# Graph attention on one core: 32x32 block transposes on VectorE, and P times V in sixteen parts of the array

## Chip, cores, metric

One core of one Trainium2 chip. The metric is device time in microseconds (us) of the whole kernel, one launch. All tensors are in float32.

## What is computed

Two layers on x (16 batches, 512 nodes, 128 features), each followed by a residual and a layer norm.

```
h = x @ fc_in_w.T + fc_in_b                      # layer 0: 8 Euler steps on the graph
8 times: h = h + dt * (sigmoid(alpha)*0.5*(adj @ h - h) + h @ w_eff - h + x)
x1 = layernorm(x + h)
q, k, v = split_heads(x1 @ W)                    # layer 1: 4 heads of 32
P = softmax(q @ k.T / sqrt(32) + mask)           # mask: adj == 0 -> -inf; 512 x 512 per head
out = layernorm(x1 + P @ v)
```

## The kernel before

The eight Euler steps are folded into powers of one 512x512 matrix that is built once, in the first 60 us. After that the kernel works on one batch per iteration, 16 iterations, two of them (j = 0 and 1, one group of two batches) in one pass of the loop over g. Four jobs are software-pipelined: an iteration runs a share of layer 0 ("HORNER" pieces XT, Z, C, BC, BM), prepares the batch of two iterations ago (LN1A, LN1B, X1T, Q, K, V and the scores S0 of head 0), does the scores and transposes (S, TR) of the batch of three iterations ago, and ends the batch of four iterations ago (PV, OT, CB, LN2A, LN2B, and the store). The order in which every engine takes these is one hand-written list, EVENTS (L66), and LATE_EVENTS (L87) once layer 0 is through. All engines walk the same list in order, and each has only its own part of each event.

Attention, for one head (32 columns) and one of four tiles i of 128 queries:

- `S` (scores, L648): TensorE writes 128 queries by 512 keys to psS[i % 2]. VectorE (maximum, L847) adds the mask, takes the row maximum and writes the result to Sm; ScalarE (exponential, L461) writes exp to E[:, h % 2, i], queries on the partitions.
- `TR` (L702): P times V needs keys on the partitions, so TensorE transposes four 128x128 squares of E into a bank psE; ScalarE (L514, even i) or VectorE (L886, odd i) copies the bank to ET. An iteration has 16 TR, 64 transposes in all.
- `PV` (L717): for each of four key tiles n and each head, one matmul of 128 keys by 32 columns of V against 512 queries of ET. The four heads lie in four column groups of the array (psO[rows]). A float32 matmul is two loads and two matmuls for the engine, a transpose one of each; so an iteration has 32 PV pairs of load and matmul, and 64 transpose pairs.
- `OT` and `CB` bring psO back to queries on the partitions, and scale it by the reciprocal sums.

VectorE also makes the low parts of split float32r operands (L824) and the layer norms (L826 to L843), GpSimd the inverse roots (L400). SyncE's queue loads x, stores y, and stacks Q and K parts by 24 DMAs per iteration (L345), each 64 KB. V is kept by ScalarE (L506) in two buffers V[:, j]. The loop over g from 2 to 6 is one body that is run five times; the rest is unrolled.

Of the kernel before, what the change touches and what calls it, by code (L numbers as in the profile page):

```python
# [31 lines left out]
KS = 3 * HD  # L32

# [37 lines left out]
    ("HORNER", 2, 0),  # L71
# [7 lines left out]
    ("HORNER", 6, 0),  # L79
    ("TR", 3, 0), ("TR", 3, 1), ("S0", 0, 0), ("S0", 0, 1),  # L80
    ("HORNER", 7, 0), ("V", 3, 0),
    ("TR", 3, 2), ("TR", 3, 3), ("S0", 0, 2), ("S0", 0, 3),
# [67 lines left out]
def gnn_kernel(nc, x, adj, alpha, w, d, fc_w, fc_b, w_qkv, out):  # L150
    with ExitStack() as ctx:
# [42 lines left out]
        V = sb("V", [P, 2, NT, D])  # L194
# [735 lines left out]
```

## Time and profile before

| | us |
|---|---|
| three runs | 734.71, 736.24, 736.66 (median 736.24) |
| the profiled execution, its own time | 734.45 |
| its span | 732.4 |
| TensorE matmul busy | 687.3 (94%) |
| TensorE weight load busy | 558.1 (76%) |
| VectorE busy | 417.4 (57%) |
| ScalarE busy | 380.7 (52%) |

The span is the part between the first and the last recorded instruction; some 2 us lie around it. Busy times of different engines overlap, and weight loads lie beside matmuls. What sets the time is the engine that never waits in a stretch, so stretches of one iteration are read by themselves.

### The profile page before, as it was taken

To read this page: it belongs to the slowest core of one execution; us is meant where nothing else is said; L and a number is where in the kernel's file an instruction comes from. 1 tells how busy PE (TensorE), PEld (TensorE's weight loads), DVE (VectorE), ACT (ScalarE), POOL (GpSimd) and SP (SyncE) were. 2 spreads that over 40 slices of the span, in tenths; PEclk is the share of its full clock that TensorE was granted. 3 is DMA by queue.
4 is the path that set the end of the run, shared out by engine and by line. 5 is a ranking of instruction groups with operands and counts; after the bars stand their busy time and mean duration, and the time that the engine had idled before them with its cause. 6 is when DMAs were issued, how large, how long until landed. Compare 5 with 4: busy or idle time off the path is not lost.

```text
span 732.4 us, 14091 instructions
## 1 busy us (share of the span) xinstructions
PE 687.3 (94%) x4753; PEld 558.1 (76%) x4753; DVE 417.4 (57%) x1229; ACT 380.7 (52%) x855; POOL 71.1 (10%) x85
## 2 busy tenths in 40 slices
PE   5999999999999999999999999999999999978674
PEld 3778988987888788878797788878887889654441
DVE  5440114555576475657575667557564757686863
ACT  3131124665556565556565555656456655665660
POOL 5010100201002000200020100200020000000000
PEclk9999999999999999999999999999999999997997
DMA  3000003030302221130304030312112120312210
GB/s 104 1 1 29 1 30 84 15 98 9 92 12 71 59 58 42 43 86 25 75 0 124 5 96 4 80 49 63 37 47 55 34 69 23 80 40 62 76 27 29
DMA packets 37058, 35.39 MB, mean 48 GB/s; under 512 B 7456, under 2 KB 24224, under 8 KB 37024
## 3 DMA queue, kind: packets, MB, share of 16 engines
q1 hardware_dynamic: 37024, 34.96, 18.4%
q8 instruction: 19, 0.31, 0.2%
q14 instruction: 15, 0.12, 0.1%
HBM read 5.57 MB, written 4.19 MB: 13 GB/s over the span
## 4 chain that ended last, share of the span: by engine, by line
PE 75%; DVE 7%; issue 6%; SPq 5%; DMA 4%; ACT 2%; DVEq 0%; POOLq 0%; POOL 0%; ACTq 0%
PE psL L614 12%; PE psE L714 12%; PE psO L725 8%; PE psS L654 7%; SPq L345 5%; PE psL L625 4%; PE psL L627 4%; PE psL L626 4%; PE psL L642 3%; PE psL L644 3%; PE psL L643 3%; DMA Ks<-kl 3%; PE psM L691 3%; DVE Sm L855 2%; DVE y L843 2%
## 5 line engine op out<-in xcount | busy, mean ns | idle before, releaser
L466 ACT ACTIVATE E<-Sm,negmax 128x512 f32<-128x512 f32 x256 | 182.8, 716 | 137.3 <-DVE negmax L855 137.3
L855 DVE CUSTOM_DVE_ANT_0 Sm<-psS,mask 128x512 f32<-128x512 f32 x256 | 166.3, 684 | 14.9 <-PE psS L654 9.9
L886 DVE COPY ET<-psE 128x512 f32<-128x512 f32 x116 | 79.8, 688 | 146.9 <-PE psE L714 146.8
L614 PE MATMUL psL<-R,zT 128*128 128x128 f32 x1152 | 142.1, 275 | 0.0
L714 PEld LDWEIGHTS psE<-ident,E 128*128 128x128 f32 x928 | 105.5, 143 | 44.3 <-issue 39.6
L614 PEld LDWEIGHTS psL<-R,zT 128*128 128x128 f32 x1152 | 137.0, 192 | 2.0 <-issue 0.2
L714 PE MATMUL psE<-ident,E 128*128 128x128 f32 x928 | 124.7, 278 | 2.5 <-DVE ET L886 1.5
L654 PE MATMUL psS<-Ks,Qs 96*128 96x512 f32 x256 | 96.4, 451 | 19.2 <-DVE negmax L855 9.2
L514 ACT ACTIVATE ET<-psE 128x512 f32<-128x512 f32 x116 | 68.9, 594 | 61.6 <-PE psE L714 61.4
L400 POOL TENSOR_TENSOR rstd<-var,minus_half 128x4 f32<-128x4 f32 x32 | 32.3, 1009 | 571.4 <-DVE var L838 571.4
L642 PE MATMUL psL<-Yh,PTh 128*128 128x256 f32 x256 | 72.7, 284 | 0.0
L644 PE MATMUL psL<-Yh,PTl 128*128 128x256 f32 x256 | 71.8, 281 | 0.0
L643 PE MATMUL psL<-Yl,PTh 128*128 128x256 f32 x256 | 71.8, 280 | 0.0
L725 PE MATMUL psO<-ET,V 128*32 128x512 f32 x512 | 66.0, 643 | 0.9 <-issue 0.9
L654 PEld LDWEIGHTS psS<-Ks,Qs 96*128 96x128 f32 x256 | 40.2, 192 | 32.5 <-DVE negmax L855 19.3
L824 DVE TENSOR_TENSOR Yl<-psL,Yh 128x512 fp32r<-128x512 f32 x32 | 22.1, 692 | 59.1 <-ACT Yh L459 59.1
L625 PE MATMUL psL<-PTh,Yh 128*128 128x512 f32 x128 | 52.0, 406 | 0.2 <-ACT zT L480 0.2
L627 PE MATMUL psL<-PTh,Yl 128*128 128x512 f32 x128 | 50.6, 395 | 0.0
L626 PE MATMUL psL<-PTl,Yh 128*128 128x512 f32 x128 | 50.4, 394 | 0.0
L643 PEld LDWEIGHTS psL<-Yl,PTh 128*128 128x128 f32 x256 | 48.3, 189 | 0.9
L642 PEld LDWEIGHTS psL<-Yh,PTh 128*128 128x128 f32 x256 | 48.2, 188 | 1.0
L644 PEld LDWEIGHTS psL<-Yh,PTl 128*128 128x128 f32 x256 | 48.2, 188 | 0.0
(127 smaller groups left out, 793.1 us busy)
## 6 DMA issues: line engine op xcount, KB each, us to landing
Qs<-qh SPq DMA_DIRECT2D x128, 64.0 KB, 2.0
Ks<-kh SPq DMA_DIRECT2D x128, 64.0 KB, 2.0
xin<-in_x_dram SPq DMA_DIRECT2D x8, 512.0 KB, 3.8
Qs<-ql SPq DMA_DIRECT2D x64, 64.0 KB, 2.0
Ks<-kl SPq DMA_DIRECT2D x64, 64.0 KB, 2.0
out_dram<-y SPq DMA_DIRECT2D x16, 256.0 KB, 2.3
E<-in_adj_dram SPq DMA_DIRECT2D x4, 256.0 KB, 3.5
W_sb<-in_L_gnn_W_dram SPq DMA_DIRECT2D x1, 192.0 KB, 4.1
```

The source lines that it names most:

```text
L466: nc.scalar.activation(E[:, h % 2, i, :], Sm[:, i % 2, :], ACT.Exp, scale=-1.0, bias=negmax[:, h * NT + i:h * NT + i + 1], accum_out=sums[ ...
L614: last = mm(bank_ap[:, (t * GB + b) * D:(t * GB + b + 1) * D], zT[:, i, b, nodes], R[:, block * PW + i, :], start=False, stop=alone and t ...
L625: mm(psL[n % 2][:, :], Xh[:, b, k, :], PTh[:, power_, k, :], start=k == 0, stop=False)
L627: last = mm(psL[n % 2][:, :], Xl[:, b, k, :], PTh[:, power_, k, :], start=False, stop=k == NT - 1)
L642: mm(out_ap, PTh[:, PW - 1, k, nodes], Yh[:, step, k, :], start=False, stop=False)
L643: mm(out_ap, PTh[:, PW - 1, k, nodes], Yl[:, step, k, :], start=False, stop=False)
L644: last = mm(out_ap, PTl[:, PW - 1, k, nodes], Yh[:, step, k, :], start=False, stop=(k == NT - 1 and t == TU - 1))
L654: mm(psS[i % 2][:, :], Qs[0:KS, h, i * P:(i + 1) * P], Ks[0:KS, h, :], start=True, stop=True).then_inc(s_mm, 1)
L714: last = nc.tensor.transpose(e_bank(horner, i)[:, t * P:(t + 1) * P], E[:, n % 2, t, i * P:(i + 1) * P], ident[:, :])
L725: last = mm(psO[rows, :], V[:, j, n, rows], ET[:, h, n, :], start=n == 0, stop=n == NT - 1)
L855: V_.tensor_tensor_reduce(out=Sm[:, i % 2, :], in0=psS[i % 2][:, :], in1=mask[:, i, :], scale=-SCALE, scalar=3e38, op0=ALU.add, op1=ALU.mi ...
L886: V_.tensor_copy(ET[:, n, i, :], e_bank(horner, i)[:, :]).then_inc(t_ev[1], 1)
```

## The change

E tiles are no longer transposed by TensorE. VectorE transposes each 128x512 tile of E in 32x32 blocks, SBUF to SBUF, in one instruction per TR. A block transpose leaves every block in its own 32 partitions: partition group k then holds, for all 16 blocks of 32 keys, the queries whose place in their tile of 128 is 32k to 32k+31. So PV becomes, for each of 16 key blocks b, each partition group k and each head h, one matmul of 32 keys by 32 columns against 128 queries, in the part of the array at rows k and columns h; the four k write four banks of a four-bank psO. All of PV stands at one place, in HORNER slot 0. Each group k needs all of V, so 16 DMAs on SyncE's queue copy V (one buffer now) to Vg, each 32 partitions to 32 partitions. maximum writes to E directly and ScalarE's exp works in place (Sm goes). Banks of psO stand in for psE and psM. ScalarE and VectorE no longer copy psE, and ScalarE's OT reads four banks. TR moves later in the list, and waits of its own go with it: VectorE's first TR of a batch waits for PV (o_mm), PV for all TR (t_done), for V and for its copies.

```diff
 EVENTS = [
-    ("HORNER", 0, 0), ("PV", 0, 0), ("PV", 1, 0),
-    ("TR", 0, 0), ("TR", 0, 1), ("S", 1, 0), ("S", 1, 1), ("LN1A", 0, 0),
-    ("HORNER", 1, 0), ("PV", 2, 0), ("PV", 3, 0),
-    ("TR", 0, 2), ("TR", 0, 3), ("S", 1, 2), ("S", 1, 3), ("OT", 0, 0), ("LN1B", 0, 0),
-    ("HORNER", 2, 0),
-    ("TR", 1, 0), ("TR", 1, 1), ("S", 2, 0), ("S", 2, 1), ("CB", 0, 0),
-    ("HORNER", 3, 0), ("X1T", 0, 0),
-    ("TR", 1, 2), ("TR", 1, 3), ("S", 2, 2), ("S", 2, 3), ("LN2A", 0, 0),
+    ("HORNER", 0, 0), ("PV", 0, 0), ("S", 1, 0), ("S", 1, 1), ("LN1A", 0, 0),
+    ("HORNER", 1, 0), ("OT", 0, 0), ("TR", 0, 0), ("TR", 0, 1), ("S", 1, 2), ("S", 1, 3), ("LN1B", 0, 0),
+    ("HORNER", 2, 0), ("TR", 0, 2), ("TR", 0, 3), ("S", 2, 0), ("S", 2, 1), ("CB", 0, 0),
+    ("HORNER", 3, 0), ("X1T", 0, 0), ("TR", 1, 0), ("TR", 1, 1), ("S", 2, 2), ("S", 2, 3), ("LN2A", 0, 0),
     ("HORNER", 4, 0), ("Q", 1, 0), ("QL", 1, 0),
-    ("TR", 2, 0), ("TR", 2, 1), ("S", 3, 0), ("S", 3, 1), ("LN2B", 0, 0),
-    ("HORNER", 5, 0), ("K", 2, 0), ("KL", 2, 0),
-    ("TR", 2, 2), ("TR", 2, 3), ("S", 3, 2), ("S", 3, 3),
-    ("HORNER", 6, 0),
-    ("TR", 3, 0), ("TR", 3, 1), ("S0", 0, 0), ("S0", 0, 1),
-    ("HORNER", 7, 0), ("V", 3, 0),
-    ("TR", 3, 2), ("TR", 3, 3), ("S0", 0, 2), ("S0", 0, 3),
+    ("TR", 1, 2), ("TR", 1, 3), ("S", 3, 0), ("S", 3, 1), ("LN2B", 0, 0),
+    ("HORNER", 5, 0), ("K", 2, 0), ("KL", 2, 0), ("TR", 2, 0), ("TR", 2, 1), ("S", 3, 2), ("S", 3, 3),
+    ("HORNER", 6, 0), ("V", 3, 0), ("TR", 2, 2), ("TR", 2, 3), ("S0", 0, 0), ("S0", 0, 1),
+    ("HORNER", 7, 0), ("TR", 3, 0), ("TR", 3, 1), ("S0", 0, 2), ("S0", 0, 3), ("TR", 3, 2), ("TR", 3, 3),
     ("HORNER", 8, 0),
 ]
 
...
 LATE_EVENTS = [
     ("S", 1, 0), ("S", 1, 1), ("LN1A", 0, 0), ("S", 1, 2), ("S", 1, 3),
-    ("PV", 0, 0), ("PV", 1, 0), ("PV", 2, 0), ("PV", 3, 0), ("OT", 0, 0),
-    ("TR", 0, 0), ("TR", 0, 1), ("TR", 0, 2), ("TR", 0, 3),
-    ("S", 2, 0), ("S", 2, 1), ("LN1B", 0, 0), ("S", 2, 2), ("S", 2, 3), ("CB", 0, 0),
-    ("X1T", 0, 0),
-    ("TR", 1, 0), ("TR", 1, 1), ("TR", 1, 2), ("TR", 1, 3),
-    ("Q", 1, 0), ("S", 3, 0), ("S", 3, 1), ("S", 3, 2), ("QL", 1, 0), ("S", 3, 3), ("K", 2, 0),
-    ("LN2A", 0, 0), ("KL", 2, 0),
-    ("TR", 2, 0), ("TR", 2, 1), ("TR", 2, 2), ("TR", 2, 3), ("LN2B", 0, 0),
-    ("TR", 3, 0), ("TR", 3, 1), ("TR", 3, 2), ("TR", 3, 3), ("V", 3, 0),
-    ("S0", 0, 0), ("S0", 0, 1), ("S0", 0, 2), ("S0", 0, 3),
+    ("PV", 0, 0), ("OT", 0, 0), ("TR", 0, 0), ("TR", 0, 1), ("TR", 0, 2), ("TR", 0, 3),
+    ("S", 2, 0), ("S", 2, 1), ("LN1B", 0, 0), ("TR", 1, 0), ("TR", 1, 1), ("S", 2, 2), ("S", 2, 3), ("CB", 0, 0),
+    ("X1T", 0, 0), ("TR", 1, 2), ("TR", 1, 3),
+    ("Q", 1, 0), ("S", 3, 0), ("S", 3, 1), ("QL", 1, 0), ("TR", 2, 0), ("TR", 2, 1),
+    ("K", 2, 0), ("S", 3, 2), ("S", 3, 3), ("LN2A", 0, 0), ("KL", 2, 0),
+    ("TR", 2, 2), ("TR", 2, 3), ("LN2B", 0, 0), ("V", 3, 0),
+    ("TR", 3, 0), ("TR", 3, 1), ("S0", 0, 0), ("S0", 0, 1), ("TR", 3, 2), ("TR", 3, 3), ("S0", 0, 2), ("S0", 0, 3),
     ("S0", 1, 0), ("S0", 1, 1), ("S0", 1, 2), ("S0", 1, 3),
 ]
...
-        V = sb("V", [P, 2, NT, D])
+        V = sb("V", [P, NT, D])
+        Vg = sb("Vg", [P, 2, BLOCKS, D])
 
...
-        Sm = sb("Sm", [P, 2, N])
         negmax = sb("negmax", [P, H * NT])
         E = sb("E", [P, 2, NT, N])
-        ET = sb("ET", [P, H, NT, N])
+        ET = sb("ET", [P, H, BLOCKS, NT, QUAD])
         oT = sb("oT", [P, N])
...
-        psE = [bank("psE0"), bank("psE1")]
-        psO = bank("psO")
-        psM = bank("psM")
-        R_BANKS = [psL[0], psL[1], psO]
-        P_BANKS = psS + psE
+        psO = ctx.enter_context(nc.psum_tensor("psO", [P, GROUPS, N], F32))
+        psC, psX, psQ, psK = (psO[:, k, :] for k in range(GROUPS))
+        psV, psM = psX, psK
+        R_BANKS = [psL[0], psL[1], psC]
+        P_BANKS = psS + [psX, psQ]
...
+                    sp.wait_ge(m_ev, MPB * (it - PREP) + 4)
+                    if end:
+                        sp.wait_ge(o_mm, it - END + 1)
+                    for group in range(GROUPS):
+                        for q in range(GROUPS):
+                            sp.dma_start(Vg[group * QUAD:(group + 1) * QUAD, j, q:BLOCKS:GROUPS, :],
+                                         V[q * QUAD:(q + 1) * QUAD, :, :]).then_inc(v_in[group], 16)
...
-            def exponential(a, parity, h, i, fresh):
+            def exponential(a, parity, h, i):
                 s = s_unit(a, h, i)
                 act.wait_ge(s_max, s + 1)
-                if not fresh:
-                    act.wait_ge(t_mm, s_unit(a, h - 1, 0))
-                nc.scalar.activation(E[:, h % 2, i, :], Sm[:, i % 2, :], ACT.Exp, scale=-1.0,
+                nc.scalar.activation(E[:, h % 2, i, :], E[:, h % 2, i, :], ACT.Exp, scale=-1.0,
                                      bias=negmax[:, h * NT + i:h * NT + i + 1],
                                      accum_out=sums[:, parity, h * NT + i:h * NT + i + 1]).then_inc(s_exp, 1)
...
-                        nc.scalar.activation(V[:, j, :, :], psM[:, :].rearrange("p (t d) -> p t d", d=D),
+                        for part_in in v_in:
+                            act.wait_ge(part_in, GROUPS * 16 * p)
+                        nc.scalar.activation(V[:, :, :], psV[:, :].rearrange("p (t d) -> p t d", d=D),
                                              ACT.Copy).then_inc(m_ev, 1)
...
-                    elif kind == "TR" and i % 2 == 0:
-                        act.wait_ge(t_mm, s_unit(a, n, i) + 1)
-                        nc.scalar.activation(ET[:, n, i, :], e_bank(horner, i)[:, :], ACT.Copy).then_inc(t_ev[0], 1)
...
                         act.wait_ge(o_mm, e + 1)
-                        nc.scalar.activation(oT[:, :], psO[:, :], ACT.Copy).then_inc(o_ev, 1)
+                        nc.scalar.activation(oT[:, :].rearrange("p (i k c) -> p k i c", i=NT, k=GROUPS),
+                                             psO[:, :, 0:P].rearrange("p k (i c) -> p k i c", i=NT),
+                                             ACT.Copy).then_inc(o_ev, 1)
...
                         pe.wait_ge(x1_done, p + 1)
+                        if end:
+                            pe.wait_ge(o_ev, e + 1)
...
-                    elif kind == "TR":
-                        r = s_unit(a, n, i)
-                        if i == 0:
-                            pe.wait_ge(s_exp, s_unit(a, n, NT))
-                        evacuated = (a * H + n) * (NT // 2) + i // 2
-                        if not horner and not (g == NG and j == 0 and n == 0):
-                            pe.wait_ge(t_ev[i % 2], evacuated - 1)
-                        elif not horner and i >= 2:
-                            pe.wait_ge(l0_ev[i % 2], EPB * NG)
-                        elif not isinstance(evacuated, int) or evacuated > 0:
-                            pe.wait_ge(t_ev[i % 2], evacuated)
-                        for t in range(NT):
-                            last = nc.tensor.transpose(e_bank(horner, i)[:, t * P:(t + 1) * P],
-                                                       E[:, n % 2, t, i * P:(i + 1) * P], ident[:, :])
-                        last.then_inc(t_mm, 1)
                     elif kind == "PV":
-                        if n == 0:
-                            for part_ev in t_ev:
-                                pe.wait_ge(part_ev, H * NT // 2 * (e + 1))
-                            pe.wait_ge(c_ev, e + C_FREE)
-                            pe.wait_ge(m_ev, MPB * (e + 1))
-                        for h in range(H):
-                            rows = slice(h * HD, (h + 1) * HD)
-                            last = mm(psO[rows, :], V[:, j, n, rows], ET[:, h, n, :],
-                                      start=n == 0, stop=n == NT - 1)
-                        if n == NT - 1:
-                            last.then_inc(o_mm, 1)
+                        pe.wait_ge(t_done, H * NT * (e + 1))
+                        pe.wait_ge(c_ev, e + C_FREE)
+                        pe.wait_ge(m_ev, MPB * (e + 2 if prep or attend else B))
+                        for part_in in v_in:
+                            pe.wait_ge(part_in, GROUPS * 16 * (e + 1))
+                        carry_waits(pe, pe_passed)
+                        for b in range(BLOCKS):
+                            for k in range(GROUPS):
+                                keys = slice(k * QUAD, (k + 1) * QUAD)
+                                for h in range(H):
+                                    rows = slice(h * HD, (h + 1) * HD)
+                                    last = mm(psO[rows, k, 0:P], Vg[keys, j, b, rows],
+                                              ET[keys, h, b, :, :], start=b == 0, stop=b == BLOCKS - 1)
+                        last.then_inc(o_mm, 1)
...
-                if not fresh or i >= 2:
-                    dve.wait_ge(s_exp, s - 1)
+                freed = s_unit(a, h - 2, i) + 1
+                if not isinstance(freed, int) or freed > 0:
+                    dve.wait_ge(t_done, freed)
                 carry_waits(dve, dve_passed)
 
-                V_.tensor_tensor_reduce(out=Sm[:, i % 2, :], in0=psS[i % 2][:, :], in1=mask[:, i, :],
+                V_.tensor_tensor_reduce(out=E[:, h % 2, i, :], in0=psS[i % 2][:, :], in1=mask[:, i, :],
                                         scale=-SCALE, scalar=3e38, op0=ALU.add, op1=ALU.min,
                                         accum_out=negmax[:, at:at + 1]).then_inc(s_max, 1)
...
+                    elif kind == "TR":
+                        if n == 0 and i == 0 and (not isinstance(a, int) or a > 0):
+                            dve.wait_ge(o_mm, a)
+                        dve.wait_ge(s_exp, s_unit(a, n, i) + 1)
+                        V_.transpose(ET[:, n, :, i, :],
+                                     E[:, n % 2, i, :].rearrange("p (b c) -> p b c", c=QUAD)).then_inc(t_done, 1)
```

## Rows read from the trace of the kernel before

**Rows 1.** The page: span, and busy time of each engine.
```profile
span 732.4 us, 14091 instructions
...
PE 687.3 (94%) x4753; PEld 558.1 (76%) x4753; DVE 417.4 (57%) x1229; ACT 380.7 (52%) x855; POOL 71.1 (10%) x85
```
**Rows 2.** Busy time by stretch, first line its columns: two iterations, late iterations.
```profile
core 0: us, PE busy (x) PEld busy (x) DVE busy (x) ACT busy (x) POOL busy (x), PEclk, DMA share, GB/s
395.81:435.09 39.28, 39.10 (x267) 31.22 (x270) 24.12 (x73) 23.51 (x54) 2.58 (x3) 1.00 0.23 59
435.09:474.87 39.78, 39.21 (x315) 33.83 (x318) 24.75 (x73) 22.18 (x51) 5.09 (x5) 1.00 0.18 47
633.00:663.00 30.00, 23.89 (x133) 14.95 (x133) 23.06 (x72) 20.25 (x48) 2.58 (x3) 0.90 0.22 56
663.00:695.00 32.00, 24.97 (x133) 15.12 (x132) 22.87 (x71) 19.28 (x46) 2.58 (x3) 0.87 0.23 57
695.00:732.40 37.40, 23.20 (x145) 12.01 (x144) 19.67 (x60) 13.65 (x32) 2.01 (x2) 0.82 0.11 30
```
**Rows 3.** TensorE matmuls in order: start us, us from first start to last end.
```profile
395.75 1.92 PE L725 MATMUL psO<-ET,V 128*32 128x512 f32 x16
397.60 1.09 PE L714 MATMUL psE<-ident,E 128*128 128x128 f32 x8
```
**Rows 4.** VectorE in order, same columns, in brackets idle before.
```profile
400.55 0.86 DVE L830 BATCH_NORM_STATS2 stats<-u 128x6 f32<-128x128 f32 x4
...
401.99 0.17 DVE L838 TENSOR_SCALAR var<-mv 128x4 f32<-128x4 f32 x1
...
409.46 0.69 DVE L886 COPY ET<-psE 128x512 f32<-128x512 f32 x1 [1.20 <-PE psE L714]
410.06 0.68 DVE L855 CUSTOM_DVE_ANT_0 Sm<-psS,mask 128x512 f32<-128x512 f32 x1
```
**Rows 5.** The page's costliest groups: busy us, mean ns, idle before.
```profile
L886 DVE COPY ET<-psE 128x512 f32<-128x512 f32 x116 | 79.8, 688 | 146.9 <-PE psE L714 146.8
L714 PE MATMUL psE<-ident,E 128*128 128x128 f32 x928 | 124.7, 278 | 2.5 <-DVE ET L886 1.5
```
**Rows 6.** Waits from 395.81 to 474.87 us: total us, times, longest.
```profile
DVE ql L824 <- ACT qh L459: 1.8, 2, 0.9
...
SPq L339 <- DVE y L843: 45.9, 2, 23.5
```
**Rows 7.** PV's first instructions: begun by 435.05 us, by 435.10 us.
```profile
435.02 0.64 PE L725 MATMUL psO<-ET,V 128*32 128x512 f32 x4
...
435.02 0.16 PEld L725 LDWEIGHTS psO<-ET,V 128*32 128x32 f32 x8
```
**Rows 8.** Instruction fetches: DMA queues from 0, from 235, from 567 us.
```profile
q8 instruction: 12, 0.20, 0.3%
...
q14 instruction: 1, 0.01, 0.0%
...
q8 instruction: 7, 0.11, 0.3%
```
**Rows 9.** One fetch each in 31:34 us and 233:236 us, share of 16 engines.
```profile
q8 instruction: 1, 0.02, 2.2%
...
q8 instruction: 1, 0.02, 3.1%
```
**Rows 10.** Busy time by stretch (columns of rows 2): unrolled part, one loop pass.
```profile
31.50:233.50 202.00, 197.20 (x1371) 169.72 (x1370) 89.54 (x254) 87.11 (x189) 18.58 (x18) 1.00 0.15 38
235.00:314.10 79.10, 78.25 (x574) 65.01 (x573) 48.80 (x147) 45.62 (x105) 7.67 (x8) 1.00 0.21 53
```
**Rows 11.** DMA issues: KB each, us from issue to landing.
```profile
Ks<-kl SPq DMA_DIRECT2D x64, 64.0 KB, 2.0
...
dcol<-in_L_gnn_d_dram SPq DMA_DIRECT2D x1, 0.5 KB, 2.1
```
**Rows 12.** TensorE in the last iteration, columns of rows 3.
```profile
716.87 5.95 PE L725 MATMUL psO<-ET,V 128*32 128x512 f32 x32 [0.92 <-issue]
```

More of the change, by code:

```diff
@@ L32 @@
 KS = 3 * HD
+BLOCKS = N // QUAD
+GROUPS = P // QUAD
 IPG = GB
@@ L240, in gnn_kernel @@
         pool_passed = sem("pool_passed")
+        pe_passed = sem("pe_passed")
         c_pow = sem("c_pow")
@@ L275, in gnn_kernel @@
         s_exp = sem("s_exp")
-        t_mm = sem("t_mm")
-        t_ev = [sem("t_ev0"), sem("t_ev1")]
+        t_done = sem("t_done")
+        v_in = [sem(f"v_in{k}") for k in range(GROUPS)]
         o_mm = sem("o_mm")
@@ L293, in f @@
             return ap.bitcast(F32)
-        def e_bank(horner, i):
-            return psE[i % 2] if horner else (psE + psL)[i]
         def is_last(g):
@@ L685, in iteration @@
                         pe.wait_ge(x1_done, p + 1)
+                        if end:
+                            pe.wait_ge(o_ev, e + 1)
                         for t in range(NT):
-                            last = nc.tensor.transpose(psM[:, t * P:(t + 1) * P], x1[:, t, :], ident[:, :])
+                            last = nc.tensor.transpose(psX[:, t * P:(t + 1) * P], x1[:, t, :], ident[:, :])
                         last.then_inc(m_mm, 1)
                     elif kind in ("Q", "K"):
-                        cols = slice(0, D) if kind == "Q" else slice(D, 2 * D)
-                        mm(psM[:, :], W_sb[:, cols], x1T[:, :], start=True, stop=True).then_inc(m_mm, 1)
+                        bank_ap, cols = (psQ, slice(0, D)) if kind == "Q" else (psK, slice(D, 2 * D))
+                        mm(bank_ap[:, :], W_sb[:, cols], x1T[:, :], start=True, stop=True).then_inc(m_mm, 1)
                     elif kind == "V":
@@ L695, in iteration @@
                             nodes = slice(t * P, (t + 1) * P)
-                            last = mm(psM[:, nodes], x1T[:, nodes], W_sb[:, cols], start=True, stop=True)
+                            last = mm(psV[:, nodes], x1T[:, nodes], W_sb[:, cols], start=True, stop=True)
                         last.then_inc(m_mm, 1)
@@ L732, in iteration @@
                         for t in range(NT):
-                            last = nc.tensor.transpose(psO[:, t * P:(t + 1) * P],
+                            last = nc.tensor.transpose(psC[:, t * P:(t + 1) * P],
                                                        oT[:, t * P:(t + 1) * P], ident[:, :])
@@ L845, in normalise, with maximum @@
                 return ins
-            def maximum(a, h, i, fresh):
+            def maximum(a, h, i):
                 s = s_unit(a, h, i)
@@ L877, in iteration @@
                         dve.wait_ge(m_hi, (MPB - 2) * p + n)
-                        h_, l_ = {"QL": (qh, ql), "KL": (kh, kl)}[kind]
-                        low(psM[:, :], h_[:, :], l_[:, :]).then_inc(m_ev, 1)
+                        bank_ap, h_, l_ = {"QL": (psQ, qh, ql), "KL": (psK, kh, kl)}[kind]
+                        low(bank_ap[:, :], h_[:, :], l_[:, :]).then_inc(m_ev, 1)
                     elif kind == "S":
-                        maximum(a, n, i, False)
+                        maximum(a, n, i)
                     elif kind == "S0":
-                        maximum(p, n, i, not attend)
-                    elif kind == "TR" and i % 2 == 1:
-                        dve.wait_ge(t_mm, s_unit(a, n, i) + 1)
-                        V_.tensor_copy(ET[:, n, i, :], e_bank(horner, i)[:, :]).then_inc(t_ev[1], 1)
+                        maximum(p, n, i)
+                    elif kind == "TR":
[4 more added lines that the diff above has]
+                                     E[:, n % 2, i, :].rearrange("p (b c) -> p b c", c=QUAD)).then_inc(t_done, 1)
                     elif kind == "CB":
```

12 lines of the change are left out of this document (6 added, 6 removed).

## Prediction

> **What bounds the kernel now.** The page comes first [rows 1]: TensorE's matmuls are busy 94% of the span, VectorE 57%, ScalarE 52%. Busy time by stretch says where [rows 2]. In the steady part an iteration takes 39.3 or 39.8 us, 39.55 on average, and TensorE is busy for all but 0.4 us of it; VectorE works 24.1 to 24.8 us of it. So there every microsecond that TensorE loses is gained, as long as nobody else becomes the bound. In the last 99.4 us, where layer 0 has run out, it is otherwise: TensorE is busy for 60 to 80% and VectorE for 53 to 77%, the two take turns, and the granted clock falls to a mean of 0.82 to 0.90 of 2.4 GHz. The first 118 us have no transposes and no PV.
>
> **What goes.** TensorE in order [rows 3]: sixteen PV pairs of load and matmul begin every 1.85 us (395.75 to 397.60), eight transposes take 0.85 us more. An iteration has 32 such PV pairs and 64 transposes: 3.7 and 6.8 us, 10.5 in all. By their group [rows 5] transposes are 124.7 us for 928, 0.134 each, in which the tail of the last of each run is counted; by the order it is 0.106, and I keep to that. ScalarE loses 8 copies; it was not the bound. VectorE loses 8 copies of psE.
>
> **What comes on VectorE.** 16 transposes for 8 copies of the same 128x512. The trace shows no VectorE transpose. The nearest row is the copy of such a tile: 0.69 us long, and the next instruction starts 0.60 us after it [rows 4]. I take 0.64, a little more since a block must fill before it empties. Below, nothing speaks for less than 0.60. Above, two passes per float32 element would make it 1.2. VectorE's work per iteration becomes 24.4 + 8 x 0.605 + 16 x 0.035 = 29.8 us. To it come its waits for ScalarE's high parts and its own statistics, of which I keep 1.5 (ql alone is 0.9 per iteration [rows 6]).
>
> **Where that work can lie.** This is the step that I think decides. PV now stands whole in slot 0. It waits for t_done of TR (3, 3), VectorE's last instruction of the iteration before. What VectorE has next is the maximum of S (1, 0), whose scores TensorE issues behind PV; and TR (0, 0) waits for o_mm as well. So VectorE stands still for all of PV, and an iteration is PV plus VectorE's chain. Hand-overs add 0.2 for the first scores and 0.4 for the row of waits in front of PV, which begin only when t_done is there (in the last iteration TensorE sat 0.92 us in such waits, "issue" [rows 12]). The rest of the iteration is 29.8 + 1.5 + 0.6 = 31.9 us. TensorE's own rest is 39.1 - 10.5, under 29, and hides beside it. With X for PV, an iteration takes 31.9 + X; the change breaks even in the steady part at X = 7.65.
>
> **What PV costs, X.** 16 blocks x 4 x 4 matmuls, each two pairs as before, are 512 pairs, or 1024 instructions, for 32 pairs. The lower end: four column parts take 16 pairs of 512 columns in 1.85 us, so a pair of 128 columns holds its part 0.11 us; sixteen parts with 32 pairs each need 3.5 us, 3.6 with the start. Issue needn't hinder that: at PV's start four matmuls and eight loads in different parts begin within 50 to 80 ns, a pair in at most 14 [rows 7]; 512 pairs at 7 ns, the spacing of the first four, are 3.6 us too. The upper end: pairs whose rows differ don't run together and only four columns' parts do, 128 x 0.11 = 14 us.
>
> Between them lies the supply of instructions. The trace has fetches on a queue of their own: 12 of 16 KB in the first 235 us, then none for the four repeated passes of the loop, then 7 in the unrolled end [rows 8]. In 31.5 to 233.5 us, 2741 matmuls and loads go with 12 fetches [rows 10], about 240 of them (with register instructions between) per fetch. That is one fetch per 17 us, spread evenly and not ahead in a heap: it looks like one block fetched when the block before it is entered. A fetch's transfer takes 2.2% of 16 x 3 us = 1.06 us alone and 3.1%, 1.49 us, beside other transfers [rows 9]. No row shows how long a block is on its way in all; an ordinary transfer lands 2.0 us after its issue, 2.1 even for half a KB [rows 11]. PV's 1024 instructions are a good four blocks. At the array's pace a block lasts 0.85 us, so PV would run into four edges, the first block ready, and wait three times: X = 0.85 + 3L. With L = 2.0 plus 0.3 for the traffic, 2.3, X = 7.75. The bounds of L, 1.8 and 2.8, give 6.25 and 9.25.
>
> Does it happen in the loop too? A pass has 1147 matmuls and loads now [rows 10] and was kept; it gets 1664 more, 2.4 times as many. I take it as not kept, since only 1147 were seen to be. If it is, eight PVs run at 3.6.
>
> The Trainium skill (Advanced Engine Details and Errata, ISA Cache) gives blocks of 16 KB or 256 instructions and 128 KB on TensorE, eight blocks. The trace agrees on the block; by it 2811 instructions are eleven blocks, the loop isn't kept, and the sum stays as taken.
>
> **The sum.** Twelve full iterations: 12 x (31.9 + X - 39.55) = 12 x 0.1 = +1. The one iteration with transposes but without PV: 7 us less on TensorE, some of it then bound by VectorE, -6. The end, 99.4 us now: VectorE's busy time there is 23.06 + 22.87 + 19.67 = 65.6; three iterations with 24 more tiles add 14.5. Its own waits stay, 1.5 each. From the last PV's end (722.8 [rows 12]) to the span's lie 9.6 us, about 3.9 of them VectorE's, and 0.9 in front: 6.6 more. Beside PV it can do two maxima (1.2) in three iterations and LN1A (1.6 [rows 4]) in two, 6.8. So 80.1 + 4.5 + 6.6 - 6.8 + 4X = 84.4 + 4X, at X = 7.75 115.4, +16. Together 16X - 112.8 = +11.2: 734.45 + 11.2 = 745.7 by the profiled execution, which lies 0.24% under the median; 747 against the runs. The point of no change is X = 7.0, so the sign hangs on 0.7 us of PV.
>
> **At no cost, with their cover.** The 16 copies of V: SyncE waits 23 us of each iteration for y [rows 6], so its 25 issues take under 0.67 each and 16 more under 11. They are issued behind the stacks, are used two iterations later, and would cost only if SyncE had under 11 us left. In-place exp and maximum: the wait for TR two heads back is long over. OT reads four banks with as many elements. X1T now waits for OT, which is issued two slots ahead.
>
> **Rivals.** (a) The supply keeps up, X = 3.6. For it: issue within 14 ns a pair, and no row in which a fetch holds TensorE up. Against it: 64 KB in 3.6 us is some eighty times the rate of fetches seen. 16 x 3.6 - 112.8 = -55: 681. This is the faster one; it decides from X below 7.0, a fetch below 2.05 us. (b) The loop is kept but unrolled parts aren't supplied: eight PVs 4.15 less, 714. (c) Row parts don't overlap, X = 14, so +111: 847. For it: no row of the trace has two row parts in use; against it, column parts overlap fully. (f) Issue over a long run is slower than its start: PV's first instructions had been queued, and the trace has no run of 1024 short ones. The bounds are 7 ns a pair [rows 7] and 106 [rows 3]; midway in ratio, 27 ns, X = 14 and 847 again. Against it, nothing in those rows slows by the eighth load. The Trainium skill (TensorE: Matmul & The Clock Gate, "Wait — 56ns, not 53.3ns?") says that matmuls never begin less than about 25 ns apart, which would be X = 12.8 and 829; the trace disagrees at least for four column parts, 7 ns apart. (d) VectorE's transpose is dearer. Each 0.1 us costs 1.6 us per iteration, 24 in all; at 0.8 us 786, at 1.2 some 880. (e) TensorE, now busy for less of an iteration, loses its clock as in the end, where 80% busy went with a mean of 0.90 [rows 2]. 29 us at 0.85 are 34, 2 us over VectorE's chain in twelve iterations: 772.
>
> **Chances and range.** Forecast 0.45 (722 to 772), (a) 0.20, (b) 0.08, (c) 0.06, (f) 0.06, (d) 0.10, (e) 0.05. A measurement of this kernel tells 0.3%, 2.2 us, from no change. Of the forecast's 0.45 about a quarter lies below 734 and 0.05 within 0.3%. Faster 0.11 + 0.20 + 0.08 = 0.39, same 0.05, slower 0.56. The range takes in (a), (b), (e) and the lower part of (d): 676 to 800. The forecast's own is 722 to 772.
>
> **What would show it.** PV's line has 8192 pairs, and by stretch an iteration's PV takes 7 to 8 us, in bursts of about 0.85 us with TensorE idle between, some 11 fetches per loop pass. If it takes 3.6 without gaps, (a) holds; if it is even but 13 us or longer, (c) or (f). VectorE's transposes stand at 0.6 to 0.7 us; VectorE is idle through PV and hardly else, about 80% in an iteration of 39 to 40 us. Wrong would be the whole if VectorE works beside PV, or if TensorE waits for Vg or the stacks.

## The result and the profile after

The changed kernel takes 949.85 us (median of 4 runs, 946.98 to 951.29), the kernel before 735.48: the ratio is 1.291, 95% interval 1.287 to 1.295. The forecast was 747, its range 676 to 800. The sign, to which the prediction gave 0.56, was right; the size was not.

The page of the changed kernel: span, the clock by fortieths of the span, the fetches of instructions, and the two groups of PV and the transposes (busy us, mean ns, idle before).

```profile
span 945.2 us, 27422 instructions
...
PE 749.2 (79%) x11409; PEld 610.7 (65%) x11409; DVE 489.0 (52%) x1357; ACT 309.9 (33%) x727; POOL 70.9 (7%) x85
...
PEclk9999998788859797797958788597969798555555
...
q8 instruction: 101, 1.65, 0.8%
...
L711 PE MATMUL psO<-ET,Vg 32*32 32x128 f32 x8192 | 162.2, 367 | 79.9 <-issue 71.3
...
L874 DVE STREAM_TRANSPOSE ET<-E 128x512 f32<-128x512 f32 x256 | 165.6, 686 | 35.3 <-PE psO L711 35.3
```

TensorE was busy for 94% of a span of 732.4 [rows 1] and is for 79% of a longer one. Fetches are 101 where they were 19 [rows 8]. In its sixteen PVs TensorE stands still for 79.9 us, 71.3 of them with nothing named that it waits for.

Busy time by stretch, with the columns of [rows 2]: one PV, the rest of its iteration, twelve iterations from PV to PV, and the last four PVs.

```profile
424.03:438.25 14.22, 9.54 (x514) 7.50 (x513) 0.00 (x0) 0.00 (x0) 0.00 (x0) 0.69 0.35 83
438.25:480.49 42.24, 34.70 (x215) 30.63 (x215) 29.17 (x81) 18.36 (x44) 5.05 (x5) 0.86 0.20 50
157.90:797.68 639.78, 522.05 (x8425) 435.71 (x8424) 348.39 (x979) 221.53 (x530) 43.31 (x46) 0.80 0.25 61
797.68:945.20 147.52, 84.67 (x2137) 54.40 (x2136) 78.14 (x224) 39.33 (x98) 7.17 (x8) 0.54 0.21 52
```

An iteration takes 639.78 / 12 = 53.3 us where it took 39.55. A PV takes 13.9 on average (12.7 to 14.8), and VectorE, ScalarE and GpSimd do nothing in it. The granted clock, 1.00 in [rows 2], is 0.69 in PV: TensorE falls to the lower of its two levels, 1.2 GHz, for part of it. The next PV, from 480.49 us, has it throughout (0.50).

TensorE in order through that PV, columns of [rows 3], the idle time before in brackets:

```profile
424.03 2.89 PE L711 MATMUL psO<-ET,Vg 32*32 32x128 f32 x201
428.52 2.40 PE L711 MATMUL psO<-ET,Vg 32*32 32x128 f32 x128 [1.60 <-issue]
432.52 2.80 PE L711 MATMUL psO<-ET,Vg 32*32 32x128 f32 x128 [1.60 <-issue]
436.80 1.45 PE L711 MATMUL psO<-ET,Vg 32*32 32x128 f32 x55 [1.47 <-issue]
```

This is the pattern that the prediction named: three waits in a PV, bursts between, each burst of 128 matmuls with their 128 loads, 256 instructions. Its size is not: the bursts in the middle begin every 4.0 to 4.3 us, 256 instructions each time (the first burst has what was left of one block and the whole of the next), and a burst lasts 2.4 us and more, not 0.85.

How long a burst lasts depends on the clock. Here are 128 pairs of two other PVs (columns of [rows 2]), 1.89 us long at a granted clock of 1.00 and 2.79 at 0.51:

```profile
213.07:214.96 1.89, 1.89 (x128) 1.58 (x128) 0.00 (x0) 0.00 (x0) 0.00 (x0) 1.00 0.37 90
480.49:483.28 2.79, 2.79 (x128) 2.09 (x128) 0.00 (x0) 0.00 (x0) 0.00 (x0) 0.51 0.40 98
```

A rival for the waits is traffic, since the 16 copies of V are issued while a PV runs (427.67 to 440.95 us beside the PV above). The last PV, which waited 8.67 us for VectorE, settles it:

```profile
919.82:935.18 15.36, 11.58 (x512) 8.52 (x512) 0.00 (x0) 0.00 (x0) 0.00 (x0) 0.50 0.02 4
...
919.82 2.80 PE L711 MATMUL psO<-ET,Vg 32*32 32x128 f32 x127 [8.67 <-DVE ET L874]
923.58 2.80 PE L711 MATMUL psO<-ET,Vg 32*32 32x128 f32 x128 [0.96 <-issue]
927.32 2.81 PE L711 MATMUL psO<-ET,Vg 32*32 32x128 f32 x128 [0.94 <-issue]
```

Nothing moves in it but four fetches of instructions (DMA share 0.02), and its bursts still begin every 3.75 us. So traffic adds at most some 0.5 us to a block, and the rest of the wait is there without it.

### The profile page after: what moved, and what is told of

It is laid out like the page before. It is cut to its first block, busy times and chain, and to the rows that moved or that the text cites. A ratio compares the mean times of both kernels' runs of the same rounds, so it can differ in the third digit from the quotient of the medians.

```text
span 945.2 us, 27422 instructions
## 1 busy us (share of the span) xinstructions
PE 749.2 (79%) x11409; PEld 610.7 (65%) x11409; DVE 489.0 (52%) x1357; ACT 309.9 (33%) x727; POOL 70.9 (7%) x85
## 4 chain that ended last, share of the span: by engine, by line
issue 60%; PE 23%; DVE 8%; POOL 3%; ACT 2%; DMA 2%; SPq 1%; POOLq 0%; DVEq 0%; ACTq 0%
PE psO L711 5%; PE psL L609 3%; DVE ET L874 3%; DVE E L841 3%; PE psS L649 2%; PE psS L554 1%; DMA Ks<-kl 1%; POOL rstd L396 1%; PE psL L620 1%; SPq L334 1%; PE psL L621 1%; PE psL L622 1%; POOL Yl L389 1%; PE psO L554 1%; ACT E L460 1%
## 5 line engine op out<-in xcount | busy, mean ns | idle before, releaser
L460 ACT ACTIVATE E<-E,negmax 128x512 f32<-128x512 f32 x256 | 182.9, 715 | 407.9 <-DVE negmax L841 407.2
L841 DVE CUSTOM_DVE_ANT_0 E<-psS,mask 128x512 f32<-128x512 f32 x256 | 164.2, 677 | 267.6 <-PE psS L649 266.7
L711 PE MATMUL psO<-ET,Vg 32*32 32x128 f32 x8192 | 162.2, 367 | 79.9 <-issue 71.3
L711 PEld LDWEIGHTS psO<-ET,Vg 32*32 32x32 f32 x8192 | 124.8, 124 | 112.3 <-issue 100.4
L649 PE MATMUL psS<-Ks,Qs 96*128 96x512 f32 x256 | 133.1, 596 | 78.6 <-DMA Ks<-kl 42.5
L874 DVE STREAM_TRANSPOSE ET<-E 128x512 f32<-128x512 f32 x256 | 165.6, 686 | 35.3 <-PE psO L711 35.3
L649 PEld LDWEIGHTS psS<-Ks,Qs 96*128 96x128 f32 x256 | 54.8, 234 | 136.2 <-DVE negmax L841 61.9
L637 PEld LDWEIGHTS psL<-Yh,PTh 128*128 128x128 f32 x256 | 58.7, 229 | 0.9
L460 ACT ACTIVATION_READ_ACCUMULATOR E<-E,negmax 128x1 f32 x256 | 47.8, 187 | 0.0
L474 ACT ACTIVATE zT<-psL 128x512 f32<-128x512 f32 x48 | 28.4, 594 | 46.7 <-PE psL L622 44.5
```

Of the source, the lines that this page charges most:

```text
L460: nc.scalar.activation(E[:, h % 2, i, :], E[:, h % 2, i, :], ACT.Exp, scale=-1.0, bias=negmax[:, h * NT + i:h * NT + i + 1], accum_out=sum ...
L637: mm(out_ap, PTh[:, PW - 1, k, nodes], Yh[:, step, k, :], start=False, stop=False)
L649: mm(psS[i % 2][:, :], Qs[0:KS, h, i * P:(i + 1) * P], Ks[0:KS, h, :], start=True, stop=True).then_inc(s_mm, 1)
L711: last = mm(psO[rows, k, 0:P], Vg[keys, j, b, rows], ET[keys, h, b, :, :], start=b == 0, stop=b == BLOCKS - 1)
L841: V_.tensor_tensor_reduce(out=E[:, h % 2, i, :], in0=psS[i % 2][:, :], in1=mask[:, i, :], scale=-SCALE, scalar=3e38, op0=ALU.add, op1=ALU.min,
L874: V_.transpose(ET[:, n, :, i, :], E[:, n % 2, i, :].rearrange("p (b c) -> p b c", c=QUAD)).then_inc(t_done, 1)
```

## Experiments

Ratios are to the kernel before on the same chip.

| run | us | ratio, 95% interval |
|---|---|---|
| 512 columns per matmul, a quarter of the key blocks | 756.95 | 1.030 (1.026 to 1.033) |
| half of the key blocks | 817.62 | 1.112 (1.107 to 1.118) |
| one key block | 689.50 | 0.938 (0.935 to 0.941) |
| 32 columns, all instructions | 939.71 | 1.279 (1.272 to 1.285) |
| PV in its old form, transposes on VectorE | 743.14 | 1.011 (1.008 to 1.014) |
| store of y moved | 931.20 | 1.268 (1.265 to 1.271) |
| kernel before, loop written out | 731.07 | 0.994 (0.992 to 0.996) |
| the same again | 729.23 | 0.994 (0.992 to 0.996) |
| PV in four pieces | 897.59 | 1.223 (1.220 to 1.227) |
| four pieces, store moved | 829.46 | 1.127 (1.124 to 1.131) |
| eight pieces, store moved | 884.49 | 1.205 (1.201 to 1.210) |
| one key block, store moved | 678.12 | 0.923 (0.920 to 0.925) |
| four pieces over two iterations | 776.39 | 1.059 (1.055 to 1.062) |
| changed kernel, loop written out | 923.86 | 1.260 (1.254 to 1.266) |
| four pieces over two iterations, loop written out | 739.37 | 1.006 (1.003 to 1.008) |
| and the last iterations reordered | 741.15 | 1.008 (1.006 to 1.011) |

The first five kernels, and the one with one key block and the store moved, leave out or change a part of the computation, as their texts say; the others compute all of it.

**Columns or instructions: 512 columns.** The first four runs take one factor of PV at a time.

```diff
-for b in range(BLOCKS):
+for b in range(0, BLOCKS, NT):
...
-    last = mm(psO[rows, k, 0:P], Vg[keys, j, b, rows],
-              ET[keys, h, b, :, :], ...
+    last = mm(psO[rows, k, :], Vg[keys, j, b, rows],
+              ET[keys, h, b:b + NT, :, :], ...
```

> Leaves out: each PV matmul takes 512 columns of exp instead of 128 and only every fourth key block of V is used, so PV multiplies the wrong values. The columns that stream through the array are as many as in the changed kernel; the instructions of a PV are 256 instead of 1024. Supply theory (three times in a PV, and once in front of it, TensorE waits some 3.9 us for the next 16 KB of instructions): nothing is fetched in the loop any more, a PV takes 3.6 to 4.4 us instead of 14, an iteration 36 to 40 us, the kernel 680 to 740. Array theory (parts of the array with different rows don't run together, or the array itself sets the 0.435 us per key block): the columns are the same, so a PV stays at 14 us, or falls only to 7 where the second holds, and the kernel stays above 900, or comes to some 740 to 800. Clock theory (TensorE's low clock is what costs): the same columns at the same clock, 14 us, above 900.

756.95 us. The same columns in a quarter of the instructions:

```profile
400.13 4.47 PE L711 MATMUL psO<-ET,Vg 32*32 32x512 f32 x128
```

A PV is 4.47 us long, where the array's floor of the prediction is 3.6. So all sixteen parts do work at once, rows included: neither the array nor its row parts set the 13.9. An iteration is still 40.3 us, 35.8 outside PV: the kernel is 17 us above the upper end of what was expected, and that part isn't PV's. By its time alone the run would lie in the range of the array theory's second form (740 to 800); PV's own 4.47 us, where that form had 7, exclude it.

**32 columns.** The other way round: `ET[keys, h, b, 0:1, :]`, 32 columns, for all but the first key block, every instruction kept.

> Leaves out: three quarters of the columns of all but the first key block; every instruction of PV is there. Supply theory: the instructions are as many, so a PV stays at 12.5 to 14 us and the kernel at 920 to 950. Array theory in either form: the columns are less than a third, PV takes 4 to 5 us, the kernel 790 to 820.

939.71 us: with under a third of PV's columns the kernel is 1% faster.

```profile
423.58 2.51 PE L712 MATMUL psO<-ET,Vg 32*32 32x128 f32 x201
428.19 1.67 PE L712 MATMUL psO<-ET,Vg 32*32 32x32 f32 x128 [2.09 <-issue]
431.91 1.67 PE L712 MATMUL psO<-ET,Vg 32*32 32x32 f32 x128 [2.06 <-issue]
436.19 0.81 PE L712 MATMUL psO<-ET,Vg 32*32 32x32 f32 x55 [2.60 <-issue]
```

The first three bursts are shorter, 5.9 us in all for 8.1, and the three waits longer by nearly as much, 6.8 for 4.7: the next burst begins at its time, 3.7 and 4.3 us after the one before, whatever the array does. It is the supply of instructions that sets when a burst begins. Within a burst 128 pairs with a quarter of the columns take 1.67 us, 13 ns a pair, and in this trace 1.5 to 1.9 us at either level of the clock. With 128 columns it is 1.9 us at the full clock and 2.8, 22 ns a pair, at the lower one (rows above). So the lower clock lengthens the bursts, but since the next one waits for its block anyway, only the last burst of a PV makes the PV longer, by up to 1 us.

**Half of the key blocks.** `for b in range(0, BLOCKS, 2)`.

> Leaves out: every second of the 16 key blocks of PV. A PV has 512 instructions, a pass of the loop some 1865 matmuls and loads instead of 2889. Supply theory: if the pass is now kept, a PV in the loop takes 3.5 us (8 key blocks at 0.435 us) and in the unrolled end 8 to 11; the kernel 690 to 730. If the pass is still not kept, every PV has one or two waits of 3.9 us, 7.5 to 11 us, and the kernel stands at 800 to 850. Array theory: a PV takes half of 14 us, 7, evenly and without gaps, and the kernel comes to 840 (950 - 16 x 7).

817.62 us: not kept. With 1784 matmuls and loads in its trace (the 1865 expected were too many) a pass still fetches 10 blocks (248.74 to 340.60 us); with 1273, in the run of 512 columns, none.

```profile
q8 instruction: 10, 0.16, 0.9%
...
248.74:340.60 91.86, 76.57 (x892) 64.84 (x892) 57.91 (x162) 36.90 (x88) 7.62 (x8) 0.83 0.28 69
239.63:319.08 79.45, 70.80 (x637) 57.34 (x636) 57.70 (x162) 36.81 (x89) 7.64 (x8) 0.94 0.31 79
```

A PV in the loop, with one wait, takes 5.3 to 6.8 us, less than the 7.5 expected, since the first block is often there. The Trainium skill (Advanced Engine Details and Errata, ISA Cache) gives TensorE 128 KB in lines of 16 KB or 256 instructions. By my estimate from these two figures that is eight lines. The trace agrees on the line. The 1784 are 7.0 lines, some 7.2 with the 61 waits, register and branch instructions of a pass, and a run of 7.2 lines touches eight or nine, depending on where it starts; whether a loop that touches no more than eight is kept wasn't tried.

**One key block.** `for b in range(1)`: what the rest costs.

> Leaves out: 15 of the 16 key blocks of PV, so that PV costs next to nothing (0.4 us) and what is left is the rest of an iteration. The prediction took that rest as 31.9 us, set by VectorE's chain: then the kernel comes to about 630 (734.5 + 16 x 0.4 - 112.8). In the changed kernel the rest is 39.3 us. If the surplus of 7.4 us comes from the fetches and from TensorE's low clock, it goes away with PV's instructions and the time is 630 to 660. If it comes from the copies of V on SyncE's queue, or from VectorE's transposes and waits, it stays, and the kernel comes to 740 to 760.

689.50 us, between the two. An iteration takes 36.0 us (590.59 less 158.71, over 12), 35.5 outside PV, against 31.9 forecast and 39.4 in the changed kernel (639.78 / 12 less 13.9). So of the surplus of 7.5 us 3.9 go with the instructions and 3.6 stay. VectorE's waits and work in two iterations, 408.59 to 480.26:

```profile
DVE E L841 <- PE psS L649: 8.3, 3, 3.3
DVE Yl L809 <- ACT Yh L455: 3.0, 4, 1.5
DVE ql L809 <- ACT qh L455: 1.2, 2, 1.0
...
408.59:445.76 37.17, 32.59 (x247) 28.48 (x246) 29.19 (x81) 17.51 (x43) 5.06 (x5) 0.91 0.32 79
445.76:480.26 34.50, 30.51 (x199) 25.34 (x199) 28.53 (x81) 19.30 (x46) 2.58 (x3) 0.95 0.38 97
```

VectorE works 28.9 us of an iteration (29.8 were forecast, its transposes priced right) and waits for 7.0, where 2.1 and PV's 0.5 were put down. The largest of these, 2.5 and 3.3 us, is one for the scores S0, and they wait on TensorE for the stack Ks<-kl: 6.0 us in these two iterations, 0.8 in the kernel before. The new list has brought S0 nearer to K, and six issues of 0.6 us and the store of y stand between.

**Transposes alone.** PV in its old form, on the new operands (keys and queries don't fit together):

```diff
-for b in range(BLOCKS):
-    for k in range(GROUPS):
-        keys = slice(k * QUAD, (k + 1) * QUAD)
-        for h in range(H):
+for b in range(0, BLOCKS, NT):
+        for h in range(H):
...
+            last = mm(psO[rows, 0, :], Vg[:, j, b, rows], ET[:, h, b:b + NT, :, :], ...
```

> Changes part of the computation: PV is made as before the change, 16 matmuls of 128 keys by 32 columns against 512 queries at one place in slot 0, on the operands that the changed kernel lays out, so keys and queries don't fit together. All else, VectorE's transposes and the 16 copies of V too, is that of the changed kernel: it is the transposes on VectorE alone. Supply theory: PV takes 4 us (3.7 by the rows of before) in 64 instructions, nothing waits for instructions, and the iteration is as in the run with one key block, 35.9 us, plus the 3.4 us more of PV: 39 us and 735 to 745 in all. Rival: VectorE's transposes beside a full-height PV, or the low clock, cost more by themselves: 760 or more.

743.14 us, as expected, with PV in its old form: moving the transposes to VectorE, with the list that goes with it, costs 1.1%. 207 of the 214 us come from PV's form.

**The store moved.**

```diff
-if end and (horner or not prep):
+if end and not prep:
     store()
...
-        if not horner and h == 1:
+        if end and h == (0 if horner else 1):
             store()
```

> The changed kernel, with one thing moved: SyncE issues the store of y behind the stacks of head 0 and no longer in front of them. TensorE waits 3.4 us an iteration for the last of these stacks before the first scores S0, because six issues of 0.6 us stand behind y and kl. If that wait is worth its size on the path, some 1.8 us an iteration go (three issues of Q's stacks then lie ahead of kl): 950 - 12 x 1.8 = 928. If it only hides fetches that would be waited for later, the time stays within 5 us of 950.

931.20 us, 18.7 less. In the kernel with one key block the same move gave 11.4 of the some 22 expected:

> Leaves out 15 of the 16 key blocks of PV, as in the earlier run (689.5 us), and issues the store of y behind the stacks of head 0. The wait for the stack stood on VectorE's chain as well (2.5 to 3.3 us an iteration). If the chain theory holds, 1.8 us go here too: 690 - 12 x 1.8 = 668. If it is no different, 690, then VectorE or TensorE have the wait's time elsewhere.

There VectorE's wait for scores fell from 8.3 to 5.9 us in two iterations and TensorE then waited 5.9 us for VectorE's maxima where it had waited 2.3: part of the wait is given on.

**Fetches spread out.** The kernel before with `for g in range(2, NG - 1)` in place of the loop:

> The kernel before, its loop over g written out: TensorE then fetches every one of its some 10,000 instructions, about 40 blocks of 16 KB, but spends 8 us and more on each. Supply theory (a block takes 3.9 us to come, and the next is fetched while one runs): no wait, 735 within 0.5%. Rival (each fetch costs TensorE its 2 to 4 us wherever it stands, as some edges in the loop would show): 20 fetches more, 50 to 80 us more, 785 or above.

```profile
q8 instruction: 37, 0.61, 0.4%
```

731.07 us: twice the fetches and 0.6% faster, not slower; so fetches, even twice as many, cost nothing where 256 instructions last longer than one. The second run of it, beside the last kernel below, gave the same ratio:

> The kernel before with its loop written out, once more and beside the last kernel on the same chip, as what it must be held against: 731 as in the first run, if that gain of 0.6% was real; 735 if it was not.

**PV in four pieces.** PV's key blocks 0 to 7 and 8 to 15 of heads 0 and 1, then of heads 2 and 3, in slots 0 to 3; TR (0, 0) waits for the first two pieces, TR (2, 0) for all.

```diff
+if n == 2:
+    pe.wait_ge(t_done, H * NT * (e + 1))
-for b in range(BLOCKS):
+for b in range(n % 2 * 8, n % 2 * 8 + 8):
...
-        for h in range(H):
+        for h in range(n // 2 * 2, n // 2 * 2 + 2):
```

> The changed kernel with PV in four pieces of 256 instructions, in slots 0 to 3 instead of all in slot 0; the first two pieces do heads 0 and 1, so that VectorE may transpose head 0 of the next batch behind them and has maxima between. The number of instructions is the same, and so is that of fetches. Supply theory: a piece runs over one edge of a block at most, and the block was under way while the slower HORNER matmuls before it ran. PV then costs 4 x 1.8 to 4 x 3 us, 7 to 12, and VectorE works beside it; an iteration takes 38 to 42 us, the kernel 720 to 790. If instead a PV takes 14 us wherever its pieces stand, only VectorE's idle time is regained: TensorE has 28.6 + 14 us of work, an iteration 43 to 46, the kernel 800 to 850.

897.59 us, above the forecast and above its rival (800 to 850) too, though PV did what it should. TensorE's pieces, and then its scores:

```profile
421.56 2.03 PE L717 MATMUL psO<-ET,Vg 32*32 32x128 f32 x128
427.00 2.10 PE L717 MATMUL psO<-ET,Vg 32*32 32x128 f32 x128
432.61 2.03 PE L717 MATMUL psO<-ET,Vg 32*32 32x128 f32 x128
438.09 2.03 PE L717 MATMUL psO<-ET,Vg 32*32 32x128 f32 x128
463.05 1.22 PE L651 MATMUL psS<-Ks,Qs 96*128 96x512 f32 x2 [8.82 <-DMA Ks<-kl]
```

The same 1024 instructions take 8.2 us in place of 13.9, without a stop: the waits in PV were a matter of where the instructions stand. Behind the jump back, once per pass, the first piece still waits (2.28 us at 474.30) and then takes 3.04 us at a granted clock of 0.64. But OT and LN2B came later too, and the store of y, first on SyncE's queue, now held the stacks back until 457 us (SyncE in order):

```profile
457.12 0.38 SPq L330 DMA_DIRECT2D out_dram<-y  x1
457.73 0.57 SPq L336 DMA_DIRECT2D Qs<-qh  x1
...
459.69 1.15 SPq L336 DMA_DIRECT2D Ks<-kh  x2
460.88 0.59 SPq L336 DMA_DIRECT2D Ks<-kl  x1
```

The gain had turned into this wait. With the store moved as well:

> Both edits at once: PV in four pieces, and the store of y issued behind the stacks of head 0. In the split kernel alone TensorE waited 8.8 us an iteration for the last stack, which stood on SyncE's queue behind the store and y. Theory (in the split kernel the fetches in PV cost next to nothing and this wait took the gain): it shrinks to 2 to 3 us, an iteration goes from 52.8 to 44 to 47 us, and the kernel comes to 820 to 850. Rival (the time is TensorE's supply of instructions over the whole iteration, wherever one waits): 880 to 900, as without the move.

829.46 us, 68 less, where the same edit gave 18.7 without the pieces. Eight pieces of 128 instructions over the same slots:

> As the kernel with four pieces and the store moved, but PV in eight pieces of 128 instructions over the same four slots. Supply theory: each piece is under half a block, so the first scores of a slot wait less and no piece meets an edge early; up to 2 us an iteration less than with four pieces. If four pieces hide the fetches already, the same time within 1%.

884.49 us, 55 us slower than four. This was expected by neither; the profile shows TensorE waiting 2.5 us for ScalarE's copy of psO before X1T and VectorE up to 7.1 for CB, but which of the moved pieces causes it wasn't tried.

**Four pieces over two iterations.** The pieces of heads 0 and 1 ("PA") go ahead into the iteration that makes the transposes; X1T, Q, K and V stand one slot earlier.

```diff
+("HORNER", 6, 0), ("PA", 0, 0), ("S0", 0, 0), ("S0", 0, 1), ("TR", 3, 0), ("TR", 3, 1),
...
+("HORNER", 8, 0), ("PA", 1, 0),
+("HORNER", 0, 0), ("S", 1, 0), ("S", 1, 1), ("LN1A", 0, 0), ("PV", 2, 0), ("TR", 0, 0), ("TR", 0, 1),
+("HORNER", 1, 0), ("S", 1, 2), ("S", 1, 3), ("PV", 3, 0), ("OT", 0, 0), ...
```

> The kernel with four pieces and the store moved, in another order: the pieces of heads 0 and 1 move up into slots 6 and 8 of the iteration before, behind the eviction of V and in front of the first scores S0, so that they cover the wait for the stacks; the pieces of heads 2 and 3 stand in slots 0 and 1, and VectorE may transpose head 0 of the next batch from slot 0 on. X1T, Q, K and V stand one slot earlier. Theory (what is left over the kernel before is VectorE standing still at PV, 11 us an iteration at its worst, and the wait for the stacks): VectorE has 29 us of work and TensorE 28.6 + 8.1 with some of it at the low clock; an iteration takes 39 to 43 us, the kernel 740 to 780. Rival (the fetches bound TensorE: 11.3 blocks per pass, however spread, cost as in the kernel with four pieces): 48 us an iteration, 820 to 830.

776.39 us. TensorE's longest idle time now stands behind the loop's jump back:

```profile
407.38 2.03 PE L718 MATMUL psO<-ET,Vg 32*32 32x128 f32 x128
414.36 1.01 PE L665 MATMUL psL<-ident,xin 128*128 128x128 f32 x4 [4.96 <-issue]
417.37 1.22 PE L651 MATMUL psS<-Ks,Qs 96*128 96x512 f32 x2 [1.99 <-issue]
```

Both kernels with their loop written out:

> The changed kernel with its loop over g written out. Its loop isn't kept between passes, so TensorE fetches the same number of instructions either way; what goes is the jump back at the end of a pass. Theory (the fetch after a jump starts only with the jump, and then two blocks are waited for): the fourth wait, 2.6 us in front of every second PV and longer around the jump, goes: 3 to 5 us in each of five passes, 925 to 938. Rival (this wait has another cause, as the row of waits in front of PV): 945 to 952.

> The last kernel (776 us) with its loop written out. In it TensorE stands still 4.96 us and then 1.99 us behind the jump back, with nothing in front but instructions to come. Theory as before: 5 to 7 us in each of five passes go, 741 to 751. Rival: the waits move to another edge and the time stays within 5 us of 776.

923.86 and 739.37 us: 26 and 37 us less, with 89 fetches in place of 101; both gains are slightly larger than expected. A loop of five passes jumps back four times, so it is 6.5 and 9 us for each jump. Writing out the loop of the kernel before, which was kept, gave 4 to 5 us, so about 1 us of each of these is there in a kept loop too. The changed kernel's trace has 40 waits at PV in the twelve iterations and 36, three in each PV, with the loop written out. So the jump back of a loop that isn't kept is the fourth wait, that of 2.3 to 2.6 us in front of every second PV. The Trainium skill (Runtime: NRT & Kernel Launch, Instruction fetch mechanics) says that a taken branch out of the blocks at hand forces a fetch before execution goes on; these two runs agree. The second one's page, and ten of its iterations by stretch:

```profile
span 737.9 us, 26434 instructions
...
q8 instruction: 89, 1.46, 0.9%
...
187.57:573.65 386.08, 372.00 (x7022) 319.10 (x7021) 290.82 (x811) 186.24 (x441) 38.19 (x40) 1.00 0.33 83
```

An iteration takes 38.6 us, 0.9 less than in the kernel before and 0.5 less than in that with its loop written out (391.51 us for ten); TensorE is busy for 96% of it and the clock is back at 1.00. What it gains there it loses in the last iterations, where layer 0's matmuls no longer stand between the pieces: from 684 us on four pieces take 3.0 to 4.1 us each, and the last four, in one row, 17.5 in all. Not all of that is fetches: the one at 684.35 us has no stop in it and takes 3.67 us in place of 2.03, at a granted clock of 0.50. Reordering these, with VectorE's transposes behind the pieces, gave nothing:

> The kernel of 739 us (PV in four pieces over two iterations, loop written out), with the order of the last three iterations changed: VectorE transposes head 3 behind the first piece of PV instead of waiting for scores (3.9 and 4.2 us in two iterations), Q and K stand ahead of transposes, and in the last iteration with scores the first two pieces of PV lie between transposes instead of in one row of 16 us at the end. Theory: 4 us less twice, and two pieces of 4 us less at the end, some of it taken up by VectorE's own work: 725 to 733. Rival (VectorE's work is the bound there and only moves): 737 to 741.

741.15 us: VectorE's waits of 3.9 and 4.2 us went, and others of 2.0 to 3.3 us and one of 6.2 (scores behind a piece of PV that waited 3.5 us for its copy of V) came. No version that computes all beats the kernel before, and all the less the kernel before with its loop written out.

## Why the prediction was wrong, step by step

**PV's price, X: the mechanism right, both terms mis-sized.** X was 0.85 + 3L with L = 2.3, 7.75 us. Measured is 13.9. The larger miss is L: in the steady part a block comes every 3.7 to 4.3 us, outside the bounds of 1.8 to 2.8 that I took from ordinary landings [rows 11], and three of them are over 5 us more. The other is the 0.85 for a block at the array's pace: 128 pairs take 1.9 to 2.0 us at the full clock and 2.8 at the lower one, so over a long run a pair costs 15 or 22 ns and not the 7 of the first four [rows 7]. That is rival (f) in kind, at half its 27 ns and, at the lower clock, nearer to it. (c) and (f) both had X = 14, for reasons that the runs exclude as the whole of it; that they come nearest to the measured 13.9 is chance. The row that I had, one fetch per 17 us [rows 10], bounded it only from above, and the nearest durations [rows 9, 11] were those of a transfer, not of the wait for it. By my own sum, 16X - 112.8, X = 13.9 makes 844; so this step alone is 98 of the 201 us between 745.7 and the profiled 946.98.

**The rest of an iteration: 39.4 and not 31.9.** That is 12 x 7.5 = 90 us more. The runs divide it: 3.6 us stay without PV's instructions and are waits on VectorE's chain, the one for scores held up by the stacks foremost. I had kept 1.5 for the chain's waits and nothing for the stacks, having costed the 16 copies of V on SyncE's queue, but not what moving S0 nearer to K does there. Moving the store alone gave back 1.0 to 1.6 us an iteration (11.4 and 18.7 us over twelve). Of the 3.9 that go with the instructions, 2.0 are the jump back: with the loop written out an iteration outside PV takes 37.4 us (611.76 / 12 less 13.6). The last 1.9 us stay open. They go along with a lower clock outside PV, 0.86 where the run with one key block has 0.93; whether the clock causes them wasn't priced alone. Rival (e) had the fall, at a chance of 0.05.

**The start and the end: small.** The iteration with transposes but without PV, put at -6 us, gave nothing: the first PV begins at 157.90 us, and at 157.88 in the kernel before. The end takes 147.5 us from the fourth last PV; my term 84.4 + 4X is 141.2 with the measured 14.2 for these four.

**What held.** The loop isn't kept (101 fetches; 14 a pass, where I wrote 11). PV has three waits inside. VectorE stands still for all of PV. Its transpose is 0.69 us long, 0.61 to the next, for 0.64 taken. All sixteen parts work side by side. The copies of V cost little: with all of them and PV's old form the kernel is at 743.

## What to carry to other kernels

Count instructions against their own supply: here a block of 256 TensorE instructions comes about every 4 us, so a stretch in which they average under 16 ns is bound by that whatever its arithmetic, while the same instructions among slower work cost 8 us in place of 14. Ask also whether a loop that was kept between passes still is, since each jump back then cost 6.5 to 9 us here, and about 1 in a kept loop. And when an edit's gain fails to show, look for the next queue that works in order: the pieces' gain had gone into one store at the head of SyncE's queue.

## What the hardware showed

- A block of 16 KB comes every 3.7 to 4.3 us when nothing slower lies in it, 3.75 with no other traffic at all.
- Alternating loads and matmuls in sixteen parts of 32x32: 128 pairs take 1.5 to 1.9 us (12 to 15 ns a pair) with 32 columns at either level of the clock; with 128 columns 1.9 us (15 ns) at 1.00 and 2.8 us (22 ns) at 0.50. With two of the four heads, eight parts, it is 2.03 us at 1.00 and 3.67 at 0.50.
- A loop of 1273 matmuls and loads was kept, one of 1784 was not.
- With 512 columns in sixteen parts 128 pairs take 4.47 us, 35 ns a pair: there the array is near its own pace.
- TensorE's clock, at 1.00 in the steady part before, falls in and after each such PV, in which TensorE stands still between the bursts, to a mean of 0.80 over twelve iterations, and to 0.54 in the last four PVs. With the same instructions spread, it is 1.00.
- Written out, the loop of the kernel before is 0.6% faster although TensorE then fetches every instruction.
